# TensorE waits for its own signal behind each group of matmuls in a two-layer graph network

## The chip, the cores and the metric

The kernel runs on one core of a Trainium2 chip. The metric is the device time of one launch in microseconds (us). Three runs of the kernel before took 3274.72, 3285.74 and 3316.88 us; the median is 3285.74 us.

Engines are named as in the profile: PE is TensorE's matmuls, PEld its weight loads, DVE is VectorE, ACT is ScalarE, POOL is GpSimd, SP is SyncE, which here only issues DMAs.

## The reference: two graph convolutions and a soft mixture of experts

There are 6250 nodes with 768 features and 106,250 directed edges sorted by destination (loops included). All is float32.

```python
def gcn_conv(x, edge_index, W, b, n_nodes):
    deg  = segment_sum(ones, dst);  dinv = rsqrt(deg)
    msg  = (x @ W.T)[src] * (dinv[src] * dinv[dst])[:, None]
    return segment_sum(msg, dst) + b

h = relu(gcn_conv(layernorm(x), edges, W1, b1))
x = x + gcn_conv(h, edges, W2, b2)
Xn = l2_normalize(layernorm(x));  sp = l2_normalize(slot_params) * scale   # 8 experts x 4 slots
logits = Xn @ sp;  D = softmax over nodes;  C = softmax over the 32 slots
Y = experts(D.T @ Xn)           # gelu(. @ W_down + b_down) @ W_up + b_up
x = x + C @ Y
```

## The kernel before

**Tiles.** The nodes are cut into T = 49 tiles of 128 nodes. A layer first sums the neighbours' rows of a tile and multiplies by W afterwards. The node table of the layer (already scaled by dinv) lies in HBM. A tile takes 18 gathered chunks of 128 rows (an indirect DMA of 384 KB each, line 625, issued by POOL): 12 "own" chunks, in which row p belongs to node p of the tile, and 6 "left" chunks, which hold the neighbours beyond the twelfth of any node, packed densely.

**Engines in a tile.** ACT copies the first own chunk into PSUM (`acc`, line 727). DVE adds the other chunks and the node's own row (`add_row(n)`, n = 0 to 11, line 1013), the last of them into `agg`. PE sums the left chunks into the PSUM tile `left` by a matmul with a 0/1 matrix `hot`, c = 0 to 5 (line 1227, two matmuls of 384 columns a chunk). DVE adds `left` to `agg` (line 1051, signal `agg_ready`). PE then turns `agg` by six transposes (line 1235, signal `agg_turned`), ACT copies them out (line 735, `aggT_ready`), PE multiplies by W in three parts behind the left sums c = 1, 2, 3 (line 1243, signal `dense_done`). In the profile a float32 matmul of 384 columns is two PE instructions and a transpose of 128 columns is one: a left chunk is four instructions, a part of the dense product eight, the turned sums six.

**What differs by layer.** In layer 1 PE also finds, for the tile two ahead, which left chunk belongs to which node: `find_left(t + 2)`, twelve PE instructions at line 1200 behind c = 2, signal `left_found`. DVE takes the result in six steps `pick_left` (line 948 the first), put between its adds n = 4 to 9. DVE then reads the dense product (line 1021 in layer 1, line 1026 in layer 2) behind add n = 8. In layer 2 PE turns the new rows (line 1252 behind c = 4, `x_turned`), ACT copies them out (line 747), and PE forms the logits (line 1258 behind c = 5, `logit_done`), which DVE reads at the start of the next step (line 1033, `logit_read`).

**Order.** Each engine has one instruction stream, written out by hand: five steps peeled off, a loop of two steps a turn, and the last steps peeled off. A step handles tile t in its left sums and tile t - 1 in its turned sums and dense product. PE's step is, in order: c = 0, turned sums, c = 1, dense part 1, c = 2, dense part 2, search (layer 1), c = 3, dense part 3, c = 4, turned rows (layer 2), c = 5, logits (layer 2). PE waits ahead of c = 0 for `hot_ready`, for `agg_ready` of the tile before, and for the gathered chunk; ahead of the turned sums for `scaled_ready` (layer 1) or `logit_read` (layer 2); ahead of dense part 1 for `aggT_ready`.

**Who waits for PE.** ACT for `agg_turned` and `x_turned`; DVE for `left_found`, `dense_done`, `logit_done` and the last `left_summed` of a tile; SP for `x_turned`; POOL for every second `left_summed`: it issues the gathers of a tile in three batches of six (slots 0 to 5, 6 to 11, 12 to 17), and batch r of the next tile may overwrite its slots once DVE's adds and the left sums c = 2r and 2r + 1 of this tile are done. So the gathers of batches 1 and 2 of a tile and of batch 0 of the next one often run as one row of 18.

Of the kernel before, what the change touches and what calls it, by code (L numbers as in the profile page):

```python
# [18 lines left out]
LEFT = 6  # L19
# [33 lines left out]
def build(nc, a):  # L53
# [10 lines left out]
    with ctx:  # L64
# [125 lines left out]
        def layer_sweep(eng, body, before_loop=None):  # L190

            for t in range(PEELED):
                body(0, t)
            if before_loop:
                before_loop()
            with eng.Fori(PEELED // 2, (T - LASTS) // 2) as i:
                for k in (1, 2):
                    body(i, k)
            for t in range(T - LASTS, T + 2):
                body(0, t)  # L200
# [119 lines left out]
        def over_pe(pe, l, nth, nth16, tile, tile16):  # L320

            def chunk(t, i):
                pe.wait_ge(O["idx_ready"], nth)
                pe.wait_ge(O["rows_in"], nth16)
                for h in range(2):
                    m = pe.matmul(left[:, h, 0:H], over_hot[:, :], over_rows[:, h * H:(h + 1) * H], start=True, stop=True)
                m.then_inc(O["summed"], 1)
                pe.reg_add(nth, nth, 1)
                pe.reg_add(nth16, nth16, 16)
            over_loops(pe, chunk)  # L330
# [821 lines left out]
        def _(pe):  # L1152
# [38 lines left out]
            for l in range(2):  # L1191
                S = L[l]
                work_free = S["scaled_ready" if l == 0 else "logit_read"]

                def find_left(t):
                    pe.wait_ge(S["ends_marked"], t + 1)
                    if not (isinstance(t, int) and t == 0):
                        pe.wait_ge(S["left_ready"], t)
                    for c in range(LEFT):
                        m = pe.matmul(found[:, c, :], before_end[:, c * P:(c + 1) * P], cands[:, ds(t, 1), :],  # L1200
                                      start=True, stop=True)
                    m.then_inc(S["left_found"], 1)
                if l == 0:
                    pe.wait_ge(s["fixed_ready"], 2)
                    find_left(0)
                else:
                    pe.wait_ge(L[0]["scaled_ready"], T)
                over_pe(pe, l, *counts)
                if l == 0:
                    find_left(1)  # L1210
                pe.wait_ge(S["over_done"], 1)

                def step(i, k):
                    t = 2 * i + k
                    known = isinstance(i, int)
                    b, other = k % 2, (k + 1) % 2
                    live, behind = (not known or t < T), (not known or 1 <= t <= T)
                    for c in range(LEFT):
                        if live:
                            slot = SLOT["left", c]  # L1220
                            if c == 0:
                                pe.wait_ge(S["hot_ready"], t + 1)
                                if not known or t >= 1:
                                    pe.wait_ge(S["agg_ready"], t)
                            pe.wait_ge(rows_in[slot], 16 * (t + 1 + l * T))
                            for h in range(2):
                                m = pe.matmul(left[:, h, 0:H], hot[:, b, c, :], rows[:, slot, h * H:(h + 1) * H],  # L1227
                                              start=c == 0, stop=c == LEFT - 1)
                            m.then_inc(S["left_summed"], 1)
                        if c == 0 and behind:  # L1230
                            pe.wait_ge(S["agg_ready"], t)
                            if not known or t >= 2:
                                pe.wait_ge(work_free, t - 1)
                            for kc in range(KC):
                                m = pe.transpose(work[:, kc // 3, (kc % 3) * P:(kc % 3 + 1) * P],  # L1235
                                                 agg[:, kc * P:(kc + 1) * P], ident[:, :])
                            m.then_inc(S["agg_turned"], 1)
                        if 1 <= c <= 3 and behind:
                            if c == 1:
                                pe.wait_ge(S["aggT_ready"], t)  # L1240
                            for part in range(4 * (c - 1), 4 * c):
                                kc, h = divmod(part, 2)
                                m = pe.matmul(work[:, h, 0:H], aggT[:, kc, :], WT[l][:, kc, h * H:(h + 1) * H],  # L1243
                                              start=kc == 0, stop=kc == KC - 1)
                            if c == 3:
                                m.then_inc(S["dense_done"], 1)
                        if c == 2 and l == 0 and (not known or t + 2 < T):
                            find_left(t + 2)
                        if c == 4 and l == 1 and behind:
                            pe.wait_ge(S["next_ready"], t)  # L1250
                            for kc in range(KC):
                                m = pe.transpose(work[:, kc // 3, (kc % 3) * P:(kc % 3 + 1) * P],
                                                 xs[:, other, kc * P:(kc + 1) * P], ident[:, :])
                            m.then_inc(S["x_turned"], 1)
                        if c == 5 and l == 1 and behind:
                            pe.wait_ge(S["xT_ready"], t)
                            for kc in range(KC):
                                m = pe.matmul(work[:, 1, H:H + SLOTS], xsT[:, 0, kc, :], sp_c[:, kc, :],  # L1258
                                              start=kc == 0, stop=kc == KC - 1)
                            m.then_inc(S["logit_done"], 1)  # L1260
                layer_sweep(pe, step)


# [85 lines left out]
```

## Time and profile before

| | |
|---|---|
| median of three runs | 3285.74 us |
| lowest, highest | 3274.72, 3316.88 us |
| the profiled execution's own time | 3279.59 us |
| its span | 3277.7 us |
| mean granted TensorE clock | 0.864 of full |
| layer 1 (tile steps), roughly | 250 to 1650 us |
| layer 2 (tile steps), roughly | 1690 to 3065 us |

The profile is of one execution. "Busy" is the share of the span in which an engine works on an instruction; "idle before" is the time for which it did nothing ahead of one, with the instruction, DMA or queue that ended it. "remote" there means that the semaphore which ended the wait moved at that moment, and that no instruction which signals it had ended within the last 1.5 us; "issue" means that no semaphore moved just before. The ends of matmuls are modelled.

### The profile page before, as it was taken

To read this page: it belongs to the slowest core of one execution; us is meant where nothing else is said; L and a number is where in the kernel's file an instruction comes from. 1 tells how busy PE (TensorE), PEld (TensorE's weight loads), DVE (VectorE), ACT (ScalarE), POOL (GpSimd) and SP (SyncE) were. 2 spreads that over 40 slices of the span, in tenths; PEclk is the share of its full clock that TensorE was granted. 3 is DMA by queue.
4 is the path that set the end of the run, shared out by engine and by line. 5 is a ranking of instruction groups with operands and counts; after the bars stand their busy time and mean duration, and the time that the engine had idled before them with its cause. 6 is when DMAs were issued, how large, how long until landed. Compare 5 with 4: busy or idle time off the path is not lost.

```text
span 3277.7 us, 27906 instructions
## 1 busy us (share of the span) xinstructions
PE 2310.0 (70%) x8202; PEld 1417.6 (43%) x8203; DVE 1722.2 (53%) x2241; ACT 532.4 (16%) x981; POOL 1861.8 (57%) x1854
## 2 busy tenths in 40 slices
PE   7426766666777666667757768877777777777778
PEld 7413444444444444444424445544444444444334
DVE  7644555555555555555535545545555555555315
ACT  7730000000000000000101111111111111111210
POOL 3446666666666666666556666666666666666000
PEclk9998888888888888888878878888889888888889
DMA  9487877777778777777768888888788887888358
GB/s 319 160 349 265 272 263 262 265 255 263 260 269 278 263 266 266 259 256 263 241 223 292 302 279 271 298 275 278 268 286 290 283 297 272 290 282 286 133 167 350
DMA packets 240127, 877.90 MB, mean 268 GB/s; under 512 B 64344, under 2 KB 65128, under 8 KB 240060
## 3 DMA queue, kind: packets, MB, share of 16 engines
q0 software_dynamic: 143808, 666.65, 60.1%
q1 hardware_dynamic: 68580, 168.86, 14.2%
q10 hardware_dynamic: 27692, 41.82, 3.5%
q8 instruction: 23, 0.38, 0.0%
q14 instruction: 24, 0.20, 0.0%
HBM read 832.39 MB, written 82.00 MB: 279 GB/s over the span
## 4 chain that ended last, share of the span: by engine, by line
another core or an unknown queue 30%; issue 29%; PE 16%; DVE 13%; ACT 5%; DMA 3%; POOL 2%; DVEq 1%; ACTq 0%; SPq 0%; POOLq 0%
DVE acc L1013 7%; PE work L1243 5%; PE left L1227 5%; PE left L1278 2%; POOL rows L584 2%; DVE agg L1013 1%; ACT logits L673 1%; ACT xsT L662 1%; DVE agg L1051 1%; PE work L1258 1%; PE work L1235 1%; ACT dump L637 1%; DVE before_end L941 1%; DMA rows<-in_W_up 0%
## 5 line engine op out<-in xcount | busy, mean ns | idle before, releaser
L625 POOL DMA_INDIRECT rows<-table_layer,gidx x1764 | 1770.6, 1004 | 986.2 <-issue 505.7
L1227 PE MATMUL left<-rows,hot 128*128 128x384 f32 x2352 | 1008.6, 561 | 474.3 <-DVE agg L1051 359.9
L1013 DVE TENSOR_TENSOR acc<-acc,rows 128x768 f32<-128x768 f32 x1078 | 1037.8, 963 | 78.2 <-DMA rows<-table_layer,gidx 23.5
L1243 PE MATMUL work<-WT,aggT 128*128 128x384 f32 x2352 | 855.5, 509 | 105.6 <-ACT aggT L735 79.0
L1227 PEld LDWEIGHTS left<-rows,hot 128*128 128x128 f32 x2352 | 487.2, 219 | 794.0 <-issue 575.9
L1243 PEld LDWEIGHTS work<-WT,aggT 128*128 128x128 f32 x2352 | 467.3, 200 | 459.6 <-ACT aggT L735 103.8
L948 DVE TENSOR_TENSOR pick_col<-slot_of,fixed 128x6 f32<-128x6 f32 x49 | 7.9, 162 | 586.8 <-remote 563.6
L1235 PE MATMUL work<-ident,agg 128*128 128x128 f32 x588 | 127.7, 379 | 153.5 <-issue 109.4
L1026 DVE SCALAR_TENSOR_TENSOR xs<-work,dinv,xs 128x768 f32<-128x768 f32 x49 | 49.9, 1018 | 345.2 <-PE work L1243 261.7
L1235 PEld LDWEIGHTS work<-ident,agg 128*128 128x128 f32 x588 | 108.7, 205 | 219.1 <-issue 214.7
L741 ACT ACTIVATE ynext<-hid,dinv 128x768 f32<-128x768 f32 x49 | 45.8, 935 | 942.4 <-DVE hid L1021 923.9
L735 ACT ACTIVATE aggT<-work 128x768 f32<-128x768 f32 x98 | 79.5, 811 | 562.7 <-remote 276.0
L747 ACT ACTIVATE xsT<-work 128x768 f32<-128x768 f32 x49 | 39.8, 811 | 724.2 <-issue 510.8
L1033 DVE COPY logits<-work 128x32 f32 (+1 forms) x49 | 9.3, 190 | 221.1 <-remote 202.8
L1051 DVE TENSOR_TENSOR agg<-left,agg 128x768 f32<-128x768 f32 x98 | 93.8, 957 | 55.5 <-remote 47.2
L727 ACT ACTIVATE acc<-rows 128x768 f32<-128x768 f32 x98 | 79.5, 811 | 239.7 <-DVE agg L1051 147.8
L1258 PEld LDWEIGHTS work<-sp_c,xsT 128*128 128x128 f32 x588 | 81.0, 211 | 43.3 <-ACT xsT L747 32.7
L1258 PE MATMUL work<-sp_c,xsT 128*128 128x32 f32 x588 | 79.1, 288 | 26.6 <-ACT xsT L747 21.9
L1013 DVE TENSOR_TENSOR agg<-acc,self_row 128x768 f32<-128x768 f32 x98 | 93.8, 958 | 4.4
L1167 PE MATMUL left<-rows 125*128 125x49 bf16 x850 | 79.1, 269 | 20.7 <-POOL steps_down L568 20.7
L974 DVE TENSOR_TENSOR hot<-fixed,left_node 128x768 f32<-128x768 f32 x98 | 92.9, 948 | 0.0
L1167 PEld LDWEIGHTS left<-rows 125*128 125x128 bf16 x850 | 78.3, 142 | 21.0 <-POOL steps_down L568 20.4
(290 smaller groups left out, 1376.3 us busy)
## 6 DMA issues: line engine op xcount, KB each, us to landing
self_row<-table_layer SPq DMA_DIRECT2D x98, 384.0 KB
rows<-table_layer,gidx POOLq DMA_INDIRECT x1764
xstage<-in_x SPq DMA_DIRECT2D x71, 384.0 KB
xs<-in_x SPq DMA_DIRECT2D x60, 384.0 KB
table_layer<-ynext SPq DMA_DIRECT2D x49, 384.0 KB
xnew<-xs SPq DMA_DIRECT2D x49, 384.0 KB
table_layer<-xstage ACTq DMA_DIRECT2D x41, 384.0 KB
rows<-xnew SPq DMA_DIRECT2D x38, 384.0 KB, 3.9
```

The source lines that it names most:

```text
L584: pool.indirect_dma_start(windows_i[:, t, :], None, src_windows[:, :], bass.IndirectOffsetOnAxis(ap=anchor[:, t:t + 1], axis=0), bounds_ch ...
L625: pool.indirect_dma_start(rows[:, slot, :], None, table[l][0:ROWS, :], bass.IndirectOffsetOnAxis(ap=gidx[:, k % 2, slot:slot + 1], axis=0) ...
L727: act.activation(acc[:, :, 0:H], halves(rows[:, SLOT["own", 0], :]), ACT.Copy).then_inc(S["first_copied"], 1)
L735: act.activation(halves(aggT[:, :, :].rearrange("p k n -> p (k n)")), work[:, :, 0:H], ACT.Copy).then_inc(S["aggT_ready"], 1)
L974: dve.tensor_tensor(hot[:, b, :, :], iota_ps.unsqueeze(1).to_broadcast([P, LEFT, P]), left_node[:, ds(t, 1), :].rearrange("p t c -> p (t c ...
L1013: dve.tensor_tensor(acc[:, :, 0:H] if n < OWN - 1 else halves(agg[:, :]), acc[:, :, 0:H], halves(row), ALU.add).then_inc(S["added"], 1)
L1051: dve.tensor_tensor(halves(agg[:, :]), left[:, :, 0:H], halves(agg[:, :]), ALU.add).then_inc(S["agg_ready"], 1)
L1167: m = pe.matmul(mm[:, 0, 0:T], oh_low[:, g % 2, :, j], oh_high[:, g % 2, :, j], start=(g == 0 and j == 0), stop=(g == GROUPS - 1 and j == ...
L1227: m = pe.matmul(left[:, h, 0:H], hot[:, b, c, :], rows[:, slot, h * H:(h + 1) * H], start=c == 0, stop=c == LEFT - 1)
L1235: m = pe.transpose(work[:, kc // 3, (kc % 3) * P:(kc % 3 + 1) * P], agg[:, kc * P:(kc + 1) * P], ident[:, :])
L1243: m = pe.matmul(work[:, h, 0:H], aggT[:, kc, :], WT[l][:, kc, h * H:(h + 1) * H], start=kc == 0, stop=kc == KC - 1)
L1258: m = pe.matmul(work[:, 1, H:H + SLOTS], xsT[:, 0, kc, :], sp_c[:, kc, :], start=kc == 0, stop=kc == KC - 1)
```

## The change

Behind each of seven kinds of signal that PE sends, PE now waits for that same signal before it goes on: behind the search, behind the left sums c = 1, 3 and 5, behind the turned sums, behind the last part of the dense product, behind the turned rows and behind the logits. Nothing is removed or moved, and no other engine's stream changes.

```diff
                     m.then_inc(S["left_found"], 1)
+                    pe.wait_ge(S["left_found"], t + 1)
...
                             m.then_inc(S["left_summed"], 1)
+                            if c % 2:
+                                pe.wait_ge(S["left_summed"], LEFT * t + c + 1)
...
                             m.then_inc(S["agg_turned"], 1)
+                            pe.wait_ge(S["agg_turned"], t)
...
                                 m.then_inc(S["dense_done"], 1)
+                                pe.wait_ge(S["dense_done"], t)
...
                             m.then_inc(S["x_turned"], 1)
+                            pe.wait_ge(S["x_turned"], t)
...
                             m.then_inc(S["logit_done"], 1)
+                            pe.wait_ge(S["logit_done"], t)
```

## Rows read from the trace of the kernel before

**Rows 1.** The page's first part: busy time of each engine, share of the span.
```profile
PE 2310.0 (70%) x8202; PEld 1417.6 (43%) x8203; DVE 1722.2 (53%) x2241; ACT 532.4 (16%) x981; POOL 1861.8 (57%) x1854
```

**Rows 2.** Stretches: PE, PEld, DVE, ACT, POOL busy us (count); clock, DMA share, GB/s.
```profile
350.00:1000.00 650.00, 453.40 (x1496) 278.85 (x1495) 351.45 (x529) 62.04 (x92) 412.83 (x411) 0.84 0.77 264
...
2400.00:3000.00 600.00, 459.12 (x1560) 278.45 (x1558) 326.44 (x366) 99.46 (x197) 388.07 (x388) 0.87 0.83 285
```

**Rows 3.** The waits: total us, times, longest.
```profile
DVE pick_col L948 <- remote: 563.6, 46, 12.8
...
ACT aggT L735 <- remote: 276.0, 29, 18.1
...
DVE logits L1033 <- remote: 202.8, 34, 10.5
```

**Rows 4.** Timeline of a layer 1 tile: start, us, engine, line, count [idle before].
```profile
1010.92 1.00 POOL L625 DMA_INDIRECT rows<-table_layer,gidx  x1 [5.22 <-DVE acc L1013]
...
1020.03 1.49 PE L1235 MATMUL work<-ident,agg 128*128 128x128 f32 x6
...
1021.55 0.81 ACT L735 ACTIVATE aggT<-work 128x768 f32<-128x768 f32 x1 [3.39 <-issue]
...
1022.42 2.36 PEld L1243 LDWEIGHTS work<-WT,aggT 128*128 128x128 f32 x8 [0.22 <-issue]
1022.65 2.74 PE L1243 MATMUL work<-WT,aggT 128*128 128x384 f32 x8
...
1029.10 1.42 PE L1200 MATMUL fixed<-xsT,before_end 128*128 x12
...
1030.36 1.54 PE L1227 MATMUL left<-rows,hot 128*128 128x384 f32 x4
...
1033.25 1.00 POOL L625 DMA_INDIRECT rows<-table_layer,gidx  x1 [0.30 <-issue]
...
1034.31 2.74 PE L1227 MATMUL left<-rows,hot 128*128 128x384 f32 x8
1036.45 0.16 DVE L948 TENSOR_TENSOR pick_col<-slot_of,fixed 128x6 f32<-128x6 f32 x1 [12.62 <-remote]
...
1039.41 1.00 POOL L625 DMA_INDIRECT rows<-table_layer,gidx  x1 [5.17 <-DVE acc L1013]
...
1044.71 0.96 DVE L1051 TENSOR_TENSOR agg<-left,agg 128x768 f32<-128x768 f32 x1
...
1045.92 2.92 PE L1227 MATMUL left<-rows,hot 128*128 128x384 f32 x4 [8.86 <-DVE agg L1051]
```

**Rows 5.** Timeline of a layer 2 tile, around the turned sums.
```profile
2409.89 0.85 PE L1235 MATMUL work<-ident,agg 128*128 128x128 f32 x6 [0.53 <-issue]
...
2410.57 1.46 PE L1227 MATMUL left<-rows,hot 128*128 128x384 f32 x4
...
2415.20 1.00 POOL L625 DMA_INDIRECT rows<-table_layer,gidx  x1 [0.30 <-issue]
...
2418.09 0.81 ACT L735 ACTIVATE aggT<-work 128x768 f32<-128x768 f32 x1 [9.46 <-remote]
2418.95 5.47 PE L1243 MATMUL work<-WT,aggT 128*128 128x384 f32 x8 [6.92 <-ACT aggT L735]
```

**Rows 6.** Timeline of another layer 2 tile, from c = 5 and the logits on.
```profile
1982.57 1.46 PE L1227 MATMUL left<-rows,hot 128*128 128x384 f32 x4
...
1983.86 1.42 PE L1258 MATMUL work<-sp_c,xsT 128*128 128x32 f32 x12
...
1985.44 1.00 POOL L625 DMA_INDIRECT rows<-table_layer,gidx  x1 [0.30 <-issue]
...
1988.23 0.96 DVE L1051 TENSOR_TENSOR agg<-left,agg 128x768 f32<-128x768 f32 x1 [3.57 <-remote]
1989.00 1.00 POOL L625 DMA_INDIRECT rows<-table_layer,gidx  x1 [2.56 <-remote]
...
1989.33 2.92 PE L1227 MATMUL left<-rows,hot 128*128 128x384 f32 x4 [4.04 <-DVE agg L1051]
```

## Prediction

> **What bounds the kernel now.** I read the page's first part, then the stretches, then the waits, then the timeline of single tiles. No engine is full: PE is busy for 70%, POOL 57%, DVE 53% [rows 1]. In layer 1, 411 gathers at 18 a tile in 650 us are one tile in 28.5 us, and the DMA engines are busy for 0.77 of that, 21.9 us; in layer 2, 388 in 600 us are 27.8 us a tile, with 0.83, or 23.1 us [rows 2]. So each tile holds 4 to 6 us in which nothing that is full is at work: a loop of waits.
>
> The waits name it. DVE waits 563.6 us, 46 times, for the search result at line 948, and ACT 276.0 us, 29 times, for the turned sums; DVE waits 202.8 us for the logits. All three have the releaser "remote": the signal moved long after any instruction that sends it had ended [rows 3]. In the timeline of a layer 1 tile the search ends at 1029.10 + 1.42 = 1030.52, but DVE starts at 1036.45: the signal is **5.9 us late**. The turned sums of the same tile end at 1021.52 and ACT starts at 1021.55: on time. Both have work queued behind them on PE [rows 4].
>
> What times the late signal is POOL. Its row of gathers runs from 1010.92 to 1033.25, one in 22.33 / 17 = 1.31 us, the last ending at 1034.25. The signal comes 2.2 us later; DVE makes three adds; POOL starts again at 1039.41, 28.49 us after 1010.92, and that is the tile [rows 4]. In layer 2 the same: the last gather of a row ends at 2416.20, and the turned sums, done since 2410.74, reach ACT at 2418.09, 7.3 us late and 1.9 us behind POOL's end [rows 5].
>
> **Does a wait behind the signal make it earlier?** This decides. PE now runs ahead: behind the search it issues c = 3, dense part 3, c = 4 and c = 5. If that work holds the signal back, a wait in front of it sends the signal out at once. Three things in the trace speak on it. First, in layer 2 PE had only c = 1 behind the turned sums (2410.57 to 2412.03) and then stood still for 6.92 us, with the signal still held [rows 5]. Second, in another tile c = 5 ended at 1984.03 and the logits at 1985.28; PE issued nothing until 1989.33, so its queue was empty, and yet DVE got the signal of c = 5 only at 1988.23, 4.2 us late, again 1.8 us behind POOL's last gather, which ended at 1986.44 [rows 6]. Third, the turned sums of layer 1 are on time with work queued behind them [rows 4]. An idle PE that waits for another engine is what PE would be behind the new waits, and there the signals are late as well. I take it that they stay late while POOL's row lasts.
>
> The Trainium skill, "Perfetto Trace Analysis", section Tensor Engine Instruction (MATMUL, LD_WEIGHTS), says that the update goes out when PSUM has acknowledged the group's own writes, followed only by propagation. By that rule nothing behind a group can delay its signal, a wait gains nothing, and the sum would be the price of the waits alone. The lateness of 5.9 us is nothing that this rule foresees.
>
> **The price of a wait on time.** Eight pipelined matmuls of 384 columns take 2.74 us: 0.32 apart, the last 0.49 long. After ACT's copy ended at 1021.55 + 0.81 = 1022.36 the next weight load came at 1022.42 and the matmul at 1022.65 [rows 4]. So with a wait the next matmul starts 0.49 + 0.06 + 0.23 = 0.78 behind the last instead of 0.32: **0.45 us** a wait. Layer 1 gets six a tile, layer 2 seven.
>
> **Layer 1, part by part.** Turned sums and c = 1 are ahead of the search and cost 0.9 us: it ends at 1031.4, still 5 us before 1036.4, so they are hidden. The wait behind the search now lasts until 1036.4. PE has then stood for about 5 us, and its matmuls restart at half clock as after other such idle times (c = 0 takes 2.92 us where c = 3 takes 1.54 [rows 4]): c = 3 ends at about 39.3, just as POOL needs it for its next batch at 39.41. Dense part 3 ends near 43.2. DVE wants it behind its fourth add after 36.54, at about 41, so `agg_ready` slips from 45.67 to near 48. The cover is POOL's row of 18 gathers, 23.6 us from 39.41: it wants batch 2's adds at 47.3 and batch 0's at 55.1, and both come before that, with 0.3 to 1 us to spare. So the tile stays at 28.5 us: **0 us**, and if the cover breaks, up to 1 us x 46 tiles. No DMA moves.
>
> **Layer 2.** The loop is: signal of the turned sums, ACT 0.81, dense part 1, c = 2, part 2, c = 3, its signal, POOL's 12 gathers, 1.9 us, next signal. Between the signal and c = 3 the new wait puts c = 1 behind the late signal instead of ahead of it. Before, from the signal: 0.86 + 5.47 for dense part 1 at half clock = 6.33 [rows 5]. After: 0.3 to start, c = 1 in 2.92 at half clock, 0.45, and part 1 in about 3.6 since the clock recovers on the way (it had, by c = 2, in the tile shown): 7.3. That is 1.0 us, bounds 0.5 (c = 1 spends the slow clock that part 1 would) and 1.9 (c = 1 and its wait in full). It counts in the 29 tiles with a late signal [rows 3]: 29. The waits behind c = 3, dense, turned rows, c = 5 and logits delay the next turned sums by some 3 us with c = 0 now behind the logits' signal; 2410.74 becomes 2414, still before 2418: hidden there. In the 20 tiles with a signal on time I charge three waits, 1.35 us: 27; bounds 0 and all seven, 63. The same rows hold for c = 1's signal itself: POOL is idle then, and it is on time.
>
> **Sum.** 0 + 29 + 27 = 56 us on the profiled 3279.6: 3336. That execution is 6 us below the median of three, so 3340. This case alone spans 3270 (late signals moved to a better place in POOL's row) to 3430 (46 + 55 + 63 on top). On TensorE's clock the skill's "TensorE: Matmul & The Clock Gate", HAM oscillation — how this bites in real kernels, warns of idle gaps between bursts; the halved speed after 8.86 us of idling agrees.
>
> **Rival A, faster: the waits work.** The run-ahead, or its history, holds the signals, and with shallow queues all are on time. Then in layer 1, from c = 0's start to the end of the search is 13.1 + 0.9, DVE's part from 1036.45 to 1045.67 is 9.2, pickup 0.3: 23.5, equal to POOL's 18 x 1.31 = 23.6. With 24.0 taken, 4.5 us x 46 = 207. In layer 2 PE is busy 459.12 / 21.6 = 21.3 us a tile [rows 2], plus 3.2 of waits and about 1 for copies on its path: 25.5, 2.3 x 45 = 104. Total 311: **2970**. For it: only PE's signals are late, and only PE runs ahead of its signals. Against: the idle queue in [rows 5, 6].
>
> **Rival B, clearly slower: c = 5 slides into the late time.** Its place is layer 2. POOL's second batch needs the signal of c = 5. In rows 6 that signal was late and POOL stood for 2.56 us before its second batch; in most tiles it just makes it. The waits behind c = 3, dense part and turned rows put it 1.35 us later. If from there it is held in every tile, 2.56 x 49 = 125 more: **3465**. It decides once c = 5 ends in the time in which signals are held rather than before it. Against: POOL gets a pause in which signals pass.
>
> That the change doesn't do what it says I leave without a chance: each awaited count is the one just sent.
>
> **Chances.** Forecast 0.60, A 0.27, B 0.13. Two per cent is 66 us, about what a measurement of this kernel tells from no change; its runs lie 42 us apart. Above 3351 is slower, below 3220 faster. The forecast's case gives 0.03 faster, 0.37 same, 0.20 slower. Together: faster 0.30, same 0.37, slower 0.33. The range must take in half of A and most of B's lower part: 2960 to 3440.
>
> **What would show it.** Right: DVE's wait at line 948 stays near 12 us, its releaser is still unmatched, PE idles about 5 us behind line 1200, the matmuls of line 1227 behind it take double time, and tiles of layer 1 stay at 28.5 us. In layer 2 line 1243 starts later behind ACT's copy. Wrong: line 948 starts within 0.1 us of the search's end, and POOL's idle time between rows of gathers in layer 1 goes from 5.2 us towards 0 (rival A). Rival B shows as POOL waiting over 2 us for line 1227 ahead of the second batch in most tiles.

## The result: 5% slower, and the profile after

The changed kernel takes 3459.83 us (median of four runs, 3448.64 to 3468.12) where the kernel before takes 3280.23: a ratio of 1.052, 95% interval 1.044 to 1.061 (a ratio is estimated from the single runs, so it can differ a little from that of the two medians). Run again in a later session it was 1.050 (1.044 to 1.057). Ratios use fast runs alone, those within 1.5% of the kernel's fastest, while medians are of all runs; they part only for the logits' wait alone and for the waits behind turned sums and dense product. The profiled execution took 3462.05 us, with a span of 3460.3.

The page's first part, of the changed kernel, against [rows 1]:

```profile
span 3460.3 us, 28602 instructions
...
PE 2415.4 (70%) x8202; PEld 1387.4 (40%) x8203; DVE 1728.4 (50%) x2241; ACT 534.3 (15%) x981; POOL 1853.1 (54%) x1854
```

POOL's and DVE's work is the same; PE spends 105 us more on the same 8202 instructions, at the same mean granted clock (0.862, before 0.864). About that much is what 13 waits in 49 tiles would take by themselves, if the last matmul ahead of each counts 0.49 us instead of 0.32 (an estimate, 108 us). The time that is lost is in waits. The same two stretches as in [rows 2], of the changed kernel:

```profile
350.00:1000.00 650.00, 480.96 (x1472) 267.65 (x1472) 345.54 (x520) 60.25 (x89) 400.15 (x401) 0.89 0.76 257
2400.00:3000.00 600.00, 423.53 (x1399) 243.23 (x1398) 295.95 (x331) 88.67 (x172) 345.56 (x347) 0.83 0.74 254
```

Eighteen gathers are a tile. 401 of them in 650 us are 29.2 us a tile in layer 1 (before 28.5), 347 in 600 us are 31.1 us in layer 2 (before 27.8). Times 48 that is 34 + 158 = 192 us, close to the 183 us between the two profiled spans. Counting gathers in a fixed stretch is good to about 0.3 us a tile, since POOL's rows and gaps fall differently on its edges. So here is each layer whole, by the first and last time that DVE reads its dense product (layer 1 line 1021, layer 2 line 1026), before and after:

```profile
L1021 DVE SCALAR_TENSOR_TENSOR hid<-work,dinv,bias x49: 1005/1008/1019, 300.6 to 1648.4; 128x768 f32<-128x768 f32 x49
L1026 DVE SCALAR_TENSOR_TENSOR xs<-work,dinv,xs x49: 1017/1018/1020, 1723.2 to 3059.1; 128x768 f32<-128x768 f32 x49
```

```profile
L1021 DVE SCALAR_TENSOR_TENSOR hid<-work,dinv,bias x49: 1016/1018/1020, 300.2 to 1675.9; 128x768 f32<-128x768 f32 x49
L1026 DVE SCALAR_TENSOR_TENSOR xs<-work,dinv,xs x49: 1016/1018/1020, 1752.7 to 3239.6; 128x768 f32<-128x768 f32 x49
```

Layer 1 goes from 1347.8 to 1375.7 us (+28), layer 2 from 1335.9 to 1486.9 (+151): **five sixths of the loss are in layer 2.** Below I give one measure or the other. A layer that no edit touches isn't equal from profile to profile either: layer 2 of the kernels whose only edit is in layer 1 takes 1351.8 and 1356.0 us.

The waits of the changed kernel, the three of [rows 3] first (total, times, longest):

```profile
DVE pick_col L948 <- remote: 449.7, 39, 12.4
...
ACT aggT L735 <- remote: 42.9, 3, 18.6
...
DVE logits L1033 <- remote: 370.2, 47, 10.4
...
PE left L1228 <- remote: 541.3, 89, 17.2
...
POOL rows L625 <- DVE acc L1013: 585.4, 100, 9.8
...
ACT aggT L735 <- PE work L1238: 555.0, 61, 13.9
```

Read them one by one. The search still reaches DVE only when POOL's row is over, a good 2 us behind its last gather (2.20 us in the tile of [rows 4]; 2.26 in the changed kernel's from 1040 us on); but the search itself now ends later, so that the signal is less late past its own end (1.91 us there, before 5.93). The turned sums' late signal has all but gone (29 times to 3). The logits took its place: late in 47 tiles, not 34. PE itself now waits 89 times for its own late signal ahead of a left sum, 40 times in layer 1 (161.5 us) and 49 in layer 2 (379.8). POOL's wait "for DVE's adds" has doubled from 278.3 to 585.4 us. In layer 2 it went from 37.8 to 322.1, while the wait for left sums fell from 138.2 to 31.2: POOL's gaps over 1.2 us there were 71 of 221 us in all and are 47 of 347, one in a tile, ahead of a single row of 18.

One tile of layer 2 shows how they hang together (start, us, engine, line, count, idle before):

```profile
2419.06 1.52 PE L1264 MATMUL work<-sp_c,xsT 128*128 128x32 f32 x12 [1.54 <-PE left L1228]
...
2426.38 1.00 POOL L625 DMA_INDIRECT rows<-table_layer,gidx  x1 [0.30 <-issue]
2427.73 0.19 DVE L1033 COPY logits<-work 128x32 f32 x1 [7.66 <-remote]
...
2428.31 2.92 PE L1228 MATMUL left<-rows,hot 128*128 128x384 f32 x4 [7.72 <-remote]
...
2431.03 1.10 PE L1238 MATMUL work<-ident,agg 128*128 128x128 f32 x6
...
2432.16 0.81 ACT L735 ACTIVATE aggT<-work 128x768 f32<-128x768 f32 x1 [11.11 <-PE work L1238]
2432.18 1.56 PE L1228 MATMUL left<-rows,hot 128*128 128x384 f32 x4
...
2434.61 0.99 POOL L625 DMA_INDIRECT rows<-table_layer,gidx  x1 [7.23 <-DVE acc L1013]
```

The logits end at 2420.58. DVE gets them at 2427.73, 7.15 us late, 0.35 us behind the end of POOL's last gather (2427.38). PE, which before went straight on to c = 0, turned sums and c = 1, has stood for 7.72 us; c = 0 then runs at half clock, 2.92 us. The turned sums end at 2432.13 and ACT has them at 2432.16, on time, because POOL is idle. But POOL is idle because its next batch needs c = 1, which ends at 2433.74: it stands for 7.23 us. (The profile names DVE's add as the releaser, but the three adds that this batch needs were done at 2431.68.) Here are the rows of the kernel before for the same places, in a tile [rows 5] and among the waits:

```profile
2405.78 1.42 PE L1258 MATMUL work<-sp_c,xsT 128*128 128x32 f32 x12
...
2407.81 1.55 PE L1227 MATMUL left<-rows,hot 128*128 128x384 f32 x4 [0.61 <-issue]
2409.55 0.19 DVE L1033 COPY logits<-work 128x32 f32 x1 [1.99 <-remote]
...
2418.98 1.00 POOL L625 DMA_INDIRECT rows<-table_layer,gidx  x1 [2.78 <-DVE acc L1013]
```

```profile
POOL rows L625 <- DVE acc L1013: 278.3, 69, 5.5
...
PE work L1235 <- DVE logits L1033: 41.5, 8, 9.2
```

There the logits, done at 2407.20, were 2.35 us late too, but c = 0 had started at 2407.81 without them, and POOL stood for 2.78 us. PE's work of c = 0, turned sums and c = 1 lay beside POOL's gathers; now it follows them. (c = 1's own signal was held there as well: it ended at 2412.03, and POOL started 0.89 us behind the moment at which ACT got the turned sums.)

One thing in these rows doesn't fit "held until POOL's row is over": the logits reached DVE at 2409.55, with five more gathers of the row to come (to 2416.20). That is common in the kernel before, where 25 of the 34 late logits arrived with one to five gathers of the row left. In the changed kernel it is 4 of 47.

### The profile page after: what moved, and what is told of

Read it like the earlier page. It is cut to its first block, busy times and chain, and to the rows that moved or that the text cites. A ratio compares the mean times of both kernels' runs of the same rounds, so it can differ in the third digit from the quotient of the medians.

```text
span 3460.3 us, 28602 instructions
## 1 busy us (share of the span) xinstructions
PE 2415.4 (70%) x8202; PEld 1387.4 (40%) x8203; DVE 1728.4 (50%) x2241; ACT 534.3 (15%) x981; POOL 1853.1 (54%) x1854
## 3 DMA queue, kind: packets, MB, share of 16 engines
q0 software_dynamic: 143808, 666.65, 57.2%
## 4 chain that ended last, share of the span: by engine, by line
PE 64%; another core or an unknown queue 18%; issue 5%; DVE 4%; POOL 3%; ACT 3%; DMA 2%; DVEq 0%; SPq 0%; ACTq 0%; POOLq 0%
PE left L1228 27%; PE work L1247 25%; PE work L1238 3%; PE work L1264 2%; PE fixed L1200 2%; PE left L1285 2%; DVE acc L1013 2%; POOL rows L584 1%; ACT logits L673 1%; ACT xsT L662 1%; PE work L1257 1%; DVE agg L1051 1%; POOL rows L625 1%; DMA rows<-in_W_up 0%
## 5 line engine op out<-in xcount | busy, mean ns | idle before, releaser
L625 POOL DMA_INDIRECT rows<-table_layer,gidx x1764 | 1761.8, 999 | 1169.8 <-DVE acc L1013 585.4
L1228 PE MATMUL left<-rows,hot 128*128 128x384 f32 x2352 | 1038.8, 574 | 695.5 <-remote 541.3
L1247 PE MATMUL work<-WT,aggT 128*128 128x384 f32 x2352 | 878.6, 519 | 90.9 <-remote 62.9
L1228 PEld LDWEIGHTS left<-rows,hot 128*128 128x128 f32 x2352 | 472.5, 216 | 1090.4 <-issue 572.5
L1247 PEld LDWEIGHTS work<-WT,aggT 128*128 128x128 f32 x2352 | 457.6, 202 | 511.6 <-PE left L1228 136.3
L1033 DVE COPY logits<-work 128x32 f32 (+1 forms) x49 | 9.4, 191 | 374.1 <-remote 370.2
L1238 PE MATMUL work<-ident,agg 128*128 128x128 f32 x588 | 110.9, 342 | 2.6 <-issue 2.2
L1264 PEld LDWEIGHTS work<-sp_c,xsT 128*128 128x128 f32 x588 | 69.5, 192 | 91.3 <-remote 62.7
L1021 DVE SCALAR_TENSOR_TENSOR hid<-work,dinv,bias 128x768 f32<-128x768 f32 x49 | 49.9, 1018 | 101.3 <-PE work L1247 101.2
```

The lines of the kernel that those rows point to most:

```text
L625: pool.indirect_dma_start(rows[:, slot, :], None, table[l][0:ROWS, :], bass.IndirectOffsetOnAxis(ap=gidx[:, k % 2, slot:slot + 1], axis=0) ...
```

## The experiments

**Theory 1**, held signals: a signal of PE that ends late in POOL's row of gathers reaches nobody until the row is at or near its end; a wait doesn't send it earlier, it makes the work behind it late too. **The rival**, bubbles: each wait has a price of its own, and thirteen in a pair of tiles (one of each layer) add up. Each kernel is the one before with the edit shown, unless said otherwise; all ratios are to the kernel before in the same session.

### Which wait costs

**All waits but the one behind the logits.**

```diff
                             m.then_inc(S["logit_done"], 1)
-                            pe.wait_ge(S["logit_done"], t)
```

> The changed kernel without its wait behind the logits; the other six kinds stay. Theory 1 (the logits' signal is held until POOL's row of gathers ends, and the wait puts c = 0, the turned sums and c = 1 behind it, for which POOL then stands idle about 7 us a tile): layer 2 goes back to about 28 us a tile, 3280 + 28 for layer 1 = 3290 to 3330 us, and POOL's idle time ahead of a row in layer 2 falls under 4 us. Theory 2 (it is the sum of the bubbles, 0.45 us for each of the seven waits of a layer 2 tile, 0.45 x 7 x 49 = 154 us): only 22 us of it goes away, 3438 us.

Measured 3406.21 us, 1.0377 (1.0358 to 1.0397). Layer 2 came down from 31.1 to 600 / 361 x 18 = 29.9 us a tile, layer 1 stayed at 29.2. Neither number was met: the logits' wait is worth some 50 us on top of the others, not all. The standing that is left in layer 2 (1418.7 us whole, +83) is mostly ahead of c = 1, behind the turned sums' held signal (18 times, 75.0 us), and ahead of the turned sums, until DVE has read late logits (14 times, 88.5 us; before 8 times, 41.5).

**The wait behind the logits alone.**

```diff
                             m.then_inc(S["logit_done"], 1)
+                            pe.wait_ge(S["logit_done"], t)
```

> The kernel before with the wait behind the logits alone. Theory 1: layer 2 tiles of 30 to 31.5 us, 3280 + 100 to 150 = 3380 to 3430 us, PE idle 7 to 9 us behind the logits. Theory 2: 49 bubbles of 0.45 us, 3302 us.

Four runs from 3375.89 to 3438.49 us, median 3426.98; the ratio, from the two shorter ones, is 1.0341 (1.0266 to 1.0415). The profile is of a longer one, 3437.8 us, at a granted clock of 0.830; the shorter two have 0.835 and 0.843, the kernel before at least 0.860. The waits of this profile:

```profile
DVE logits L1033 <- remote: 416.7, 44, 11.1
...
PE left L1227 <- remote: 492.1, 44, 12.1
```

The wait is in 49 tiles, and in 44 of them PE stood for 492.1 / 44 = 11.2 us, where a bubble would be under half a microsecond. Layer 1 is untouched (414 gathers, 28.3 us a tile). As theory 1 has it: in 40 of the 44 the signal came only with POOL's last gather of the row or behind it, most often 11.4 us late. Part of that is the place: with the wait, POOL issues rows of 18 in layer 2 and the logits end 14.1 us into one, before mostly 6.4 us into a row of 12. In the kernel before, four logits ended 14.4 to 14.6 us into a row, and they were as late, 11.2 to 11.5 us, with no wait behind them. Alone this wait costs 112 us by the interval's middle, the other waits together 124 us, all of them 172: the losses don't add. A reason that fits, not tested by itself, is that each wait moves where the next signal falls in POOL's row.

**The wait behind the search alone.**

```diff
                     m.then_inc(S["left_found"], 1)
+                    pe.wait_ge(S["left_found"], t + 1)
```

> The kernel before with the wait behind the search alone (layer 1). If a signal comes on time once nothing is queued behind it: DVE's wait at line 948 ends 5.6 us earlier in 46 tiles, over 150 us faster, under 3130 us. If the signal is held while POOL gathers, whatever is queued: DVE's wait is as long as before (its start 4.8 to 6.5 us behind the search's end), layer 1 tiles of 28.5 us, 3275 to 3300 us.

Measured 3329.11 us, 1.0155 (1.0122 to 1.0188). The signal is not prompt (4.32 us late in the tile below), so it speaks for held signals and against the rival that waits help; but the time is above what I expected. Layer 1 whole takes 1375.6 us, +28, or 0.6 us a tile; the other 20 us are in layer 2 (1356.0 against 1335.9), where nothing was edited, and I can't assign them. The tile shows where the first part comes from:

```profile
1049.30 1.42 PE L1200 MATMUL fixed<-xsT,before_end 128*128 x12
...
1055.04 0.16 DVE L948 TENSOR_TENSOR pick_col<-slot_of,fixed 128x6 f32<-128x6 f32 x1 [10.69 <-remote]
...
1055.06 2.93 PE L1228 MATMUL left<-rows,hot 128*128 128x384 f32 x4 [4.33 <-remote]
...
1058.85 1.00 POOL L625 DMA_INDIRECT rows<-table_layer,gidx  x1 [6.07 <-DVE acc L1013]
```

c = 3, which POOL's batch also needs, starts with the late signal and runs at half clock: it ends at 1057.99, and POOL starts 0.86 us behind that, 3.81 us behind the signal. Before, it was DVE's second add behind the signal that POOL waited for (done at 1038.62), 39.41 - 36.45 = 2.96 us behind the signal [rows 4]; the third was still running.

**The wait behind the turned rows alone** (`pe.wait_ge(S["x_turned"], t)`).

> The kernel before with one wait added, behind the turned rows of layer 2. Theory 1 (a PE signal that ends while POOL issues a row of gathers is held until behind the row's end, and a wait on it holds the work behind it, which here is c = 5, whose signal POOL's second batch needs): with every wait but the logits' the trace showed PE standing 3 to 4 us ahead of c = 5 behind this signal, and POOL 3 to 4 us ahead of its second batch. So this wait alone should bring most of the 83 us that layer 2 grew by in that run: 3330 to 3370 us. Rival (the waits cost their bubbles of 0.45 us each, and the sum of several makes the loss): one bubble in 49 tiles, at most 22 us, 3280 to 3305.

Measured 3300.49 us, 1.0063 (1.0032 to 1.0094). Here the rival's number was met and mine was not: alone, PE stood behind this signal only 6 times, 25.1 us in all. My expectation had misread the kernel with all waits but the logits'. PE stands 63 times ahead of a left sum in it, but 43 of them are in layer 1, 18 behind the turned sums, and only 2 (7.8 us) ahead of c = 5 behind the turned rows. The same wait is dear in a kernel below (POOL's pauses added to the changed kernel), where it stands 44 times, 267.6 us: it depends on where the signal falls.

**The waits behind left sums, turned sums and dense product.**

> The kernel before with the waits behind every second left sum, the turned sums and the dense product; none behind the search, the turned rows and the logits. Theory 1: the work behind these signals is either not needed soon or the signals are on time; 3280 to 3320 us. Rival (bubbles): five waits of 0.45 us a tile in both layers, with half of the tiles on the path, 3350 to 3390.

Measured 3368.29 us, 1.0297 (1.0255 to 1.0339): dearer than I expected.

```profile
PE work L1246 <- remote: 199.2, 65, 4.4
...
PE work L1237 <- DVE logits L1033: 91.7, 12, 9.4
```

In 65 steps the dense product's matmuls stood behind a left sum's own held signal, 3.1 us each; 56 of them are in layer 1, which grew by only 14 us (1362.0). Layer 2 grew by 53 (1388.6). There, in 12 steps the turned sums stood until DVE had read late logits; PE had waited for `logit_read` at this place before the change too, 8 times. In 18 the logits' matmuls stood behind c = 5's signal (55.0 us), in 9 c = 1 behind the turned sums' (48.4 us). So the number of the bubbles was met by other means: these are waits of 3 to 8 us in some tiles, not 0.45 us in each.

**The waits behind turned sums and dense product alone.**

> The waits behind the turned sums and the dense product alone. Where the kernel before takes about 3280 us: if c = 1's held signal carries the cost of the three kinds together, 3280 to 3310; rival (0.45 us and more for each wait), 3340 to 3370. On a chip with prompt signals: no change again.

Four runs, 3292.0, 3324.57, 3347.91 and 3357.34 us, against a median of 3279.66; the spread left no interval. The two shorter ones, which alone are compared, are 12 and 45 us above the kernel before and don't decide between my range and the rival's. The profile is of 3324.57. Layer 1 didn't change (412 gathers, 28.4 us a tile), so two bubbles in each of its tiles are hidden there; layer 2 has 367 gathers, 29.4 us (whole 1386.8, +51). The row `PE work L1235 <- DVE logits L1033` went from 41.5 us in 8 tiles to 153.7 in 22, and PE stood 10 times, 64.6 us, ahead of c = 1 behind the turned sums' signal. So c = 1 doesn't carry it all, as I had expected: the wait that was there already, for the logits' reader, is longer too. How the 51 us divide between the two is not shown.

### Is it POOL that holds the signals?

**Thin gathers.** Each gather fetches 128 instead of 768 columns, from other places; five sixths of the neighbour sums' data are left out.

```diff
-                                rows[:, slot, :], None, table[l][0:ROWS, :],
+                                rows[:, slot, 0:P], None,
+                                table[l][:, :].rearrange("r (s d) -> (r s) d", s=KC)[0:ROWS, :],
```

> The kernel before, but each gather of the tile steps fetches 128 columns of a row instead of 768, from other places of the table (it leaves out five sixths of each row's sum): the same number of indirect DMAs and of descriptors, a sixth of the bytes. It tells what holds PE's signals. If it is POOL's work on the row of gathers: the search's signal is still 4 to 7 us late and comes about 2 us behind the last gather of a row. If it is the traffic on the DMA engines: the search's signal comes within 0.1 us of the search's end in most tiles, and DVE's wait at line 948 falls from 12.6 us to about 7.

One run, 3284.74 us; the kernel before took 3282.63. Two rows of this kernel, its stretch in layer 1 and its wait for the search:

```profile
350.00:1000.00 650.00, 461.13 (x1523) 284.16 (x1522) 351.47 (x529) 62.03 (x92) 416.72 (x414) 0.85 0.23 68
```

```profile
DVE pick_col L949 <- remote: 552.7, 45, 12.6
```

The DMA engines' share fell from 0.77 to 0.23, and neither the tile (28.3 us) nor the lateness moved (before, DVE waited 563.6 us, 46 times [rows 3]). The packets of POOL's queue fell too, from 143808 to 59136; the gathers stayed as many. What holds the signals is not the bytes.

**A pause of POOL in layer 1.** PE is as before; POOL waits for the search in the middle of its row of 18.

```diff
                         for slot in range(r * CHUNKS // BATCHES, (r + 1) * CHUNKS // BATCHES):
+                            if l == 0 and slot == 3 and (not known or t >= 1):
+                                pool.wait_ge(S["left_found"], min(t + 2, T) if known else pause_needed)
+                                if not known:
+                                    pool.reg_add(pause_needed, pause_needed, 1)
```

> The kernel before, unchanged on PE; in layer 1 POOL waits for the next tile's search result in the middle of its row of 18 gathers, ahead of the fourth gather of the first batch. Theory 1 (it is POOL's unbroken row of gathers that holds the signal, and a pause of POOL lets it pass): the search is reported within 2.5 us of its end instead of 6, POOL's pause is 1 to 3 us but its 5.2 us at the batch boundary shrink, and the tile of layer 1 goes from 28.5 to 25 to 27 us: 3160 to 3240 us. Rival (the signal has a delay of its own of about 6 us, whatever POOL does): POOL stands about 6 us more in each tile and the row's boundary gets it back only in part, 3330 to 3500.

Measured **3198.79 us, 0.975** (0.971 to 0.979). A tile of its layer 1:

```profile
1035.15 1.42 PE L1205 MATMUL fixed<-xsT,before_end 128*128 x12
...
1036.60 1.00 POOL L630 DMA_INDIRECT rows<-table_layer,gidx  x1 [0.30 <-issue]
...
1040.28 0.16 DVE L953 TENSOR_TENSOR pick_col<-slot_of,fixed 128x6 f32<-128x6 f32 x1 [10.76 <-remote]
...
1041.04 1.00 POOL L630 DMA_INDIRECT rows<-table_layer,gidx  x1 [3.45 <-remote]
```

POOL's last gather ends at 1037.60 and the signal is there at 1040.28, 2.7 us later, with three gathers of the batch still to come. In the 45 tiles with a late signal it is 2.0 to 2.8 us behind POOL's last gather in nearly all, wherever in the row the search ended. Stopping POOL sends the signal; PE did nothing differently. The pause costs POOL 3.45 us but saves the 5.2 us at the row's end [rows 4]: 441 gathers in 650 us, 26.5 us a tile.

**The same in layer 2, for the turned sums** (ahead of slot 14, on `agg_turned`).

> The kernel before, unchanged on PE; in layer 2 POOL waits for the tile's turned sums in its third batch, ahead of the third gather. Theory 1: turned sums reach ACT within 2.5 us of their end in all tiles, POOL's pause is 0 to 2 us, and the loop of layer 2 gets shorter by 1 to 2.5 us a tile: 3170 to 3250 us. Rival (own delay of the signal): the pause lasts as long as the lateness of before, up to 7 us in 29 tiles, 3350 to 3450.

Measured 3295.02 us, 1.0045 (1.0018 to 1.0072). The turned sums did come on time (ACT waited for them from "remote" 2 times, 22.1 us), but now it is the turned rows' signal that is late, in 34 tiles, by up to 8.0 us (ACT stands for 574.6 us ahead of it, most of which it would stand anyway). In 31 of them it came with one to five gathers of the row still to issue. A pause frees the signals that ended before it; the next row of 16 gathers delays others.

**The changed kernel with POOL's pauses** for the search (as above) and, in layer 2 ahead of the third batch, for the logits of the tile before.

> The changed kernel with POOL's two pauses (layer 1 for the search ahead of the fourth gather of a tile's first batch, layer 2 for the logits of the tile before ahead of the third batch). Where the kernel before takes about 3280 us. Theory 1 (what costs is that PE stands behind a signal that POOL's gathers hold): logits within 3 us of their end instead of 7, the tile of layer 2 from 31.2 to 27.5 to 29.5 us, that of layer 1 from 29.1 to about 27; 3220 to 3330 us. Rival: the pauses come on top, 3500 and more. On a chip with prompt signals: no change again.

The changed kernel in the same session:

> The changed kernel once more, beside the three below. Theory 1 (the waits cost only where signals are held): where the kernel before takes about 3280 us, 1.045 to 1.06 of it; on a chip where it takes about 2810 us and signals are prompt, 0.998 to 1.004 of it. Rival (the waits have a price of their own, 0.45 us each, 13 a tile pair): there also 1.01 to 1.05.

3448.82 us without the pauses, 1.0504 (1.0444 to 1.0565); **3389.98 with them**, 1.0345 (1.0302 to 1.0388). The waits of the kernel with the pauses:

```profile
PE left L1237 <- remote: 359.4, 72, 12.9
...
POOL rows L634 <- PE work L1273: 347.3, 47, 9.0
...
DVE logits L1042 <- PE work L1273: 72.7, 49, 4.0
```

As theory 1 says, the logits are no longer held once POOL stands still (72.7 / 49 = 1.5 us of waiting, releaser matched in all 49 tiles). But the gain is 59 us, not the 120 and more that I expected: of the 72 stands ahead of a left sum, 44 (267.6 us) are in layer 2 ahead of c = 5, behind the turned rows' held signal, and POOL stands for 347.3 us until c = 5 and the logits are through.

**Both pauses on the kernel before.**

> The kernel before on PE with both pauses of POOL. Where the kernel before takes about 3280 us: if the pause pays in layer 2 too, 3120 to 3180; rival (the turned sums, 2 to 3 us behind the pause, are held by the next gathers and the pause comes on top), 3200 to 3290. On a chip with prompt signals: no change again.

Measured 3192.88 us, **0.974** (0.970 to 0.977), the fastest of the kernels whose kernel before takes 3280; against the pause in layer 1 alone the second brings nothing that can be told (the rival's case).

### The same kernels where signals are prompt

In one session the kernel before took 2810.11 us (25 runs, 2806.28 to 2814.03) instead of 3280. The changed kernel with pauses, the pauses alone, and the two waits alone ran there:

> The changed kernel with all its waits on PE, and two waits of POOL: in layer 1 for the search ahead of the fourth gather of a tile's first batch, in layer 2 for the logits of the tile before ahead of the third batch. Theory 1 (the cost of the waits is the time that PE stands behind a signal that POOL's gathers hold): with POOL still, the logits are reported within 3 us of their end instead of 7 us, c = 0 and c = 1 start 4 us earlier, and the tile of layer 2 goes from 31.2 to 27.5 to 29.5 us, that of layer 1 from 29.1 to about 27: 3220 to 3330 us. Rival (the lateness belongs to the signal or to PE's waits, not to POOL): the pauses come on top, 3500 us and more.

> The kernel before on PE, with both pauses of POOL and no wait on PE. If a pause pays in layer 2 as it did in layer 1 (28.5 to 26.6 us a tile), the time goes below 3199 us, the time with the pause in layer 1 alone: 3120 to 3180. Rival: in layer 2 the turned sums, which end 2 to 3 us behind the pause, are held by the next gathers as before, and the pause of 2 to 3 us a tile comes on top: 3200 to 3290.

> The kernel before with the waits behind the turned sums and the dense product alone. Held-signal theory (of the 88 us that the left sums', turned sums' and dense waits cost together, the part of c = 1 carries them: its own signal is held and dense part 1 stands behind it): 3280 to 3310 us. Rival (each wait costs its own 0.45 us and more, whatever is held): two waits in 49 tiles of both layers, 88 us, 3340 to 3370.

Measured 1.0002 (0.9992 to 1.0011), 1.0001 (0.9991 to 1.0010) and 0.9994 (0.9984 to 1.0003). The first of them, with **all seven kinds of wait and both pauses**:

```profile
PE 2312.9 (82%) x8202; PEld 1328.4 (47%) x8203; DVE 1733.7 (62%) x2241; ACT 530.3 (19%) x981; POOL 1855.1 (66%) x1854
```

```profile
350.00:1000.00 650.00, 563.60 (x1818) 318.06 (x1817) 429.50 (x641) 75.55 (x112) 498.15 (x499) 0.94 0.92 320
```

```profile
912.20 1.42 PE L1209 MATMUL fixed<-xsT,before_end 128*128 x12
...
913.66 0.16 DVE L957 TENSOR_TENSOR pick_col<-slot_of,fixed 128x6 f32<-128x6 f32 x1 [3.42 <-PE fixed L1209]
913.68 0.94 PEld L1237 LDWEIGHTS left<-rows,hot 128*128 128x128 f32 x4 [0.17 <-PE fixed L1209]
```

The search reaches DVE 0.04 us behind its end, in the middle of POOL's gathers, and POOL, which had the result in time, doesn't stand at its pause. 499 gathers in 650 us are 23.4 us a tile, which is POOL's 18 x 1.30: POOL issues without a gap and at the same pace as before, the DMA engines are busier (0.92, before 0.77), and yet no signal is held. So POOL's gathers alone don't hold signals.

Where no signal is held, the waits cost at most 0.1%, with the pauses in place (which alone change nothing, 1.0001); the changed kernel without them was not run there. This speaks against the rival, but not for every case: POOL is the bound here, so bubbles on PE are hidden behind it, and the run doesn't show that they would be hidden where PE's chain sets the time. The stronger answer is the 11.2 us of standing above. It also means that the expected numbers of these three, which were for held signals, don't apply. What differs between the sessions I don't know. The one with the changed kernel run again (before: 3279.66 us) has the same chip number as this one, ten minutes apart, so the number of the chip doesn't tell the two apart.

## Why the prediction was wrong

- **The bound, the held signals: right in the main.** Signals are late while POOL gathers, with PE busy or idle. A wait alone never made the search prompt, a pause of POOL brought it forward. But "late while POOL's row lasts" was too strict: in the kernel before, 25 of 34 late logits came before the row was over.
- **Layer 2: the step that failed** is "The waits behind c = 3, dense, turned rows, c = 5 and logits delay the next turned sums by some 3 us with c = 0 now behind the logits' signal; 2410.74 becomes 2414, still before 2418: hidden there." It priced the logits' wait as a bubble in a chain. But the logits end inside POOL's row of twelve, in which [rows 5] show a signal held for 7.3 us and [rows 3] the logits themselves late in 34 tiles. I had both rows and did not put the wait on them. Measured: PE stands 7.7 us ahead of c = 0, the turned sums end at 2432.13 instead of before POOL's end at 2427.38, and c = 1, on which POOL's next batch depends, right behind them at 2433.74. That is 151 us in layer 2 (158 by the stretches), where I had 56; the logits' wait alone costs 112.
- **That POOL's second dependence, c = 1, moves with it** was not seen: I had c = 1 behind the turned sums' late signal (1.0 us in 29 tiles), a case that nearly disappeared (29 tiles to 3), since the turned sums now end while POOL is idle.
- **Layer 1 at 0 us: mis-sized.** The sum said that c = 3 ends at 39.3 "just as POOL needs it for its next batch at 39.41". POOL starts 0.86 us behind the matmuls' end, so it needs them at 38.55. Where c = 3 runs at half clock, POOL's row starts 3.81 us behind the signal and no longer 2.97, as in about two thirds of the changed kernel's tiles (in the others c = 3 takes 1.56 us and nothing is lost). In place of 0 that is 28 us over layer 1, 0.6 us a tile, and the same for the search's wait alone. I had named 1 us x 46 as the case if the cover breaks. (Also, POOL starts behind two of DVE's adds, not three; this changes no term.)
- **The top of the case was added up wrong.** 46 + 55 + 63 on top of 3279.6 is 3444, not 3430. The measured time lies above either.
- **The price of a wait: 0.45 us was a little high.** In the changed kernel's layer 1 a dense part without a wait behind it starts at 1044.82 and the next group at 1047.40, 2.58 later; with one, 1052.37 and 1055.27, 2.90: 0.32 us. It is not what decided: 0.13 us less on each wait would have moved the sum down.
- **Rival A** (2970, signals prompt) had the mechanism wrong, since waits don't make signals prompt. But its picture of layer 1 with prompt signals holds: 23.4 us a tile where it had 24.0. For layer 2 it had 25.5; that is 23.4 as well, which is why the whole comes to 2810 us and not 2970.
- **Rival B** (3465) had the place, layer 2, and nearly the amount. Its rule, that a signal which slides into the held time costs POOL microseconds in every tile, is what happened, to the logits rather than to c = 5. Its sign, POOL waiting for left sums ahead of the second batch in most tiles, did not show: that wait fell from 138.2 to 31.2 us in layer 2. So the nearness of its 3465 to the 3459.83 measured is luck in part. I gave it 13% because I looked for the danger at c = 5's signal only.

The Trainium skill's rule in "Perfetto Trace Analysis", section Tensor Engine Instruction (MATMUL, LD_WEIGHTS), that an update goes out once PSUM has acknowledged the group's own writes, with only propagation behind it, fits the session with prompt signals, 0.04 us. It does not account for the lateness in the others. The measurement decides, and there are both.

## What to carry to other kernels

Before adding a wait on an engine's own signal, look up for each such signal when its consumers really start, not when the work ends; a wait behind a signal that is on time cost a third of a microsecond here, one behind a late signal made everything queued behind it as late as the signal. Ask of every group behind the wait who needs it: here it was one left sum on which POOL's next batch hung. And if a signal is late while another engine does something regular, pause that other engine as a test: one wait in POOL's stream gave 2.5%, while seven kinds of wait on PE's cost 5%. Both hold only where signals were held.

## What was not expected of the hardware

- With POOL issuing gathers without a gap, PE's signals reach other engines late: the logits by 7.15 us in the tile shown and by 11.4 us in most tiles of the kernel with the logits' wait alone. In layer 1 the search's comes 2.0 to 2.8 us behind POOL's last gather in nearly every tile. It is not the gathers' data (a sixth of the bytes, same lateness). Which part of POOL's issuing holds them stays open.
- Not every signal in a row is held: the turned sums of layer 1, which end about 10.6 us into the row of 18, are on time [rows 4]; the search, 19.6 us into it, is not. Place alone is not the rule: in layer 2 the logits were late that ended 6.4 us into a row (2400.84 to 2407.20). And a late signal need not wait for the row's end: these logits came 2.35 us late with five gathers to go, while those that ended some 14 us into a row of 18 came over 11 us late, behind its end. Where the border lies and what decides it I have not measured.
- The whole effect can be absent: the same kernel took 2810 us in one session and about 3280 in four others, though POOL issued its gathers at the same 1.30 us. What switches it stays open. A change that is worth 2.6% in the one is worth nothing in the other, and a comparison across sessions would have shown 14% for no change at all.
